# Mixer stage: the scan's result kept token-major until gated, with an order of work of its own for each engine

## The reference

```
x = x + 0.5 * ffn0(layernorm(x));  x = x + attention(layernorm(x));  x = x + 0.5 * ffn0(layernorm(x))
x = x + 0.5 * experts(layernorm(x))          # 8 experts, weighted by how often a gate chooses each
x = x + mixer(layernorm(x))
x = x + 0.5 * experts(layernorm(x))
```

```
proj = x @ W_in                  # split into z (256), x_raw (512), B (128), C (64), dt, lam, theta
x_raw = silu(x_raw); B, C = rms-normed, rotated by angles that are a running sum of dt * theta
y = y_intra + y_inter            # products within a chunk, and with the state carried from chunk to chunk
y = rms(y * silu(z))             # rms over the 256 inner features of a token
return y @ W_out
```

## Time and profile before

| | us |
|---|---|
| three runs: lowest, median, highest | 2490.32, 2500.99, 2504.65 |
| the profiled execution, its own time | 2492.45 |
| its span, first to last instruction | 2490.3 |

### The profile page before, as it was taken

How to read it: one execution, slowest core, us unless ns; L and a number is a source line. 1 busy time by engine, 2 the same in 40 slices (tenths; PEclk the granted TensorE clock), 3 DMA queues, 4 the chain that set the end, 5 groups by cost and what they waited for, 6 DMA issues and landing times. The chain is left out here.

```text
span 2490.3 us, 39953 instructions
## 1 busy us (share of the span) xinstructions
PE 2152.8 (86%) x14226; PEld 986.3 (40%) x14226; DVE 1827.8 (73%) x4240; ACT 1408.9 (57%) x2651; POOL 1448.4 (58%) x1264
## 2 busy tenths in 40 slices
PE   3689889989989989989999998479899898998778
PEld 1223233333333333333333322246566566665534
DVE  5777777777777777777777772368888888887668
ACT  2166666566566566566567566254655555556234
POOL 3366666665675665675665645146556565656358
PEclk9699999999999999999999999699999999999789
DMA  3221121212112112112112110100000000000033
GB/s 118 55 49 39 35 52 43 50 37 52 43 35 64 31 35 65 31 35 64 31 45 50 43 57 9 34 14 22 27 23 26 23 27 22 23 18 18 10 103 109
DMA packets 86599, 103.70 MB, mean 42 GB/s; under 512 B 10241, under 2 KB 68737, under 8 KB 86273
## 3 DMA queue, kind: packets, MB, share of 16 engines
q1 hardware_dynamic: 86400, 101.16, 15.5%
HBM read 29.55 MB, written 20.97 MB: 20 GB/s over the span
## 5 line engine op out<-in xcount | busy, mean ns | idle before, releaser
L386 DVE TENSOR_REDUCE mS<-ps 128x1 f32<-128x512 f32 x1024 | 672.1, 683 | 248.9 <-PE ps L758 243.5
L545 ACT ACTIVATE pr<-ps 128x512 f32<-128x512 f32 x1024 | 586.1, 598 | 382.3 <-PE ps L742 365.7
L615 POOL TENSOR_TENSOR prs<-pr 128x512 f32<-128x512 f32 x384 | 487.1, 1289 | 226.2 <-ACT pr L545 226.2
L758 PE MATMUL ps<-kst,qst 96*128 96x512 f16 x1024 | 393.1, 392 | 64.5 <-DVE mS L386 55.7
L742 PE MATMUL ps<-qst,kst 97*128 97x512 f16 x1024 | 388.7, 387 | 37.1 <-ACT pr L545 35.5
L780 PE MATMUL ps<-pr,vt 128*32 128x512 f32 x2048 | 279.2, 618 | 0.0
L742 PEld LDWEIGHTS ps<-qst,kst 97*128 97x128 f16 x1024 | 97.8, 98 | 372.5 <-ACT pr L545 229.8
L619 POOL TENSOR_TENSOR terms<-terms 128x512 f32<-128x512 f32 x128 | 162.7, 1271 | 99.9 <-DVE terms L379 99.9
L624 POOL TENSOR_TENSOR lo<-terms,hi 128x512 f16<-128x512 f32 x128 | 147.8, 1155 | 81.8 <-ACT hi L525 81.8
L379 DVE TENSOR_TENSOR terms<-ps,shared 128x512 f32<-128x512 f32 x256 | 172.1, 679 | 26.1 <-POOL lo L624 19.8
L758 PEld LDWEIGHTS ps<-kst,qst 96*128 96x128 f16 x1024 | 100.7, 98 | 222.1 <-DVE mS L386 156.2
(11 more groups left out here) (267 smaller groups left out, 4386.6 us busy)
## 6 DMA issues: line engine op xcount, KB each, us to landing
qst<-hi SPq DMA_DIRECT2D x128, 128.0 KB, 2.4
kst<-hi SPq DMA_DIRECT2D x128, 128.0 KB, 2.4
qst<-lo SPq DMA_DIRECT2D x64, 128.0 KB, 2.4
kst<-lo SPq DMA_DIRECT2D x64, 128.0 KB, 2.4
x<-in_q SPq DMA_DIRECT2D x16, 256.0 KB, 3.0
shared<-in_rope SPq DMA_DIRECT2D x1, 4096.0 KB, 14.1
x<-yold SPq DMA_DIRECT2D x16, 256.0 KB, 3.0
n<-kept SPq DMA_DIRECT2D x16, 256.0 KB, 2.1
```

Source lines behind the costliest of these rows:

```text
L386: v.tensor_reduce(mS[:, b % 2, t, s:s + 1], ps[:, 2 + n % 2, :], AX, ALU.max).then_inc(S["s_read"], 1)
L545: a.activation(pr[:, s % 2, g, :], ps[:, g % 2, :], ACT.Exp, scale=ATT_SCALE).then_inc(S["exp"], 1)
L615: g.tensor_tensor(prs[:, c, :], pr[:, 0, c, :], pr[:, 1, c, :], ALU.add).then_inc(S["prs"], 1)
L758: mm(ps[:, 2 + n % 2, :], qst[0:3 * DH, h, P * t:P * t + P], kst[0:3 * DH, h, :], start=True, stop=True).then_inc(S["s"], 1)
```

## The change

Between `products` and `W_out` the data path of a chunk is changed:

- `turn_y` no longer adds. GpSimd adds `pt[0]` and `pt[1]` to `own` in two additions of 128 x 256 (`join`), with a wait for its own first addition between them.
- `z` is projected token-major: `gates` on TensorE makes, for each chunk, three products of 256 columns with the tokens as the stationary operand (12 products of 256 columns a batch in place of 6 of 512), and ScalarE's silu writes `zs` token-major.
- `gated` on VectorE multiplies the joined `own` by `zs`, both in SBUF, into `yz` (two buffers).
- `squares` on ScalarE squares `yz` and sums over the free dimension in the same instruction (`accum_out`); `mean_square` on TensorE goes, and VectorE scales the sums in SBUF.
- `turn_y` is two plain transposes a chunk, and ScalarE copies their result from PSUM to `yzT` (`evacuate_y`, new, 128 x 256).

Besides, the one table becomes four, one for each engine, with places from 0 to 540 in an iteration of 420 (a place of 420 or more falls into the next iteration, so the end of a scan now lies there). Pieces that shared a slot have places of their own on each engine, and some are cut in two (`shift` / `mean_bc`, `angles` / `decays`, `rotate` / `rotate_low`, ScalarE's `decays` / `sin`, the two halves of `states`). `keep_busy` keeps its 5 + 2 products at places of its own. The number of iterations is written as 20; the last has no work left in it. The semaphores of a stage need no longer have adjoining numbers (`clear_semaphores`).

```diff
-    "wo": 1, "out": 3, "stats_gate": 3, "xn_gate": 5, "turn_gate": 15, "gate": 16, "top": 16,
-    "variants": (1, 5, 35, 38), "chunks": (2, 15, 50, 73), "states": (4, 14, 56, 72), "chunks_rest": (7, 22, 66, 74),
-    "products": (7, 22, 65, 75), "own": (1, 2, 26, 58), "own_p": (2, 7, 17, 70), "turn_y": (25, 35, 69, 77),
-    "gated": (34, 44, 73, 80), "squares": (25, 45, 66, 75), "mean": (35, 66, 77, 82), "mean_read": 82,
-    "experts": (15, 17, 22, 25, 36, 44, 59, 64), "sumT": 68, "y": 71, "stats2": 73, "xn2": 74, "turn2": 80,
-    "low2": 82, "project": (1, 2, 3, 6), "gates": 11, "shift": 7, "soft": 15, "steps": 34, "norm_bc": 15, "sums": 41,
-    "angles": 49, "weights": 56, "rotate": 65, "diagonal": 74, "diagonal_p": 71, "bt": 73, "scores": 75, "mask": 78,
+    "DVE": {"out": 150, "stats_gate": 170, "gate": 340, "top": 380, "variants": (10, 60, 110, 210),
+        "states": (30, 50, 140, 160, 260, 280, 370), "products": (120, 220, 350, 420), "gated": (200, 330, 460, 500),
+        "mean_read": 520, "experts": (20, 70, 180, 240), "low": 400, "y": 310, "stats": 320, "shift": 90, "mean_bc": 130,
+        "steps": 190, "decays": 230, "angles": 250, "weights": 270, "rotate": 290, "rotate_low": 300, "diagonal": 360, "mask": 390},
+    "ACT": {"xn_gate": 190, "turn_gate": 220, "own": (60, 130, 240, 280), "squares": (180, 270, 500, 520),
+        "evac_y": (420, 460, 510, 540), "experts": (20, 150, 170, 210), "xn": 260, "turn": 290, "project": (10, 30, 50, 70),
+        "gates": 140, "square_bc": 110, "soft": 160, "decays": 200, "sin": 230, "bt": 250},
+    "POOL": {"own": (10, 30, 130, 140), "join": (40, 100, 150, 420), "experts": (50, 80), "stats_gate": 60, "rms": 440,
+        "stats": 120, "norm_bc": 70, "rotate": 90, "diagonal": 110},
+    "PE": {"wo": 130, "turn_gate": 210, "gate": 250, "chunks": (50, 140, 220, 310), "rest": (100, 180, 290, 320),
+        "turn_y": (330, 440, 490, 530), "experts": (0, 10, 80, 150, 160, 170, 190, 240), "busy": (230, 260), "sumT": 270,
+        "turn": 340, "project": (30, 40, 60, 90), "gates": 120, "sums": 200, "bt": 280, "scores": 300},
...
+        def placed(engine, i, q):
+            def pieces(name, role):
+                at = AT[engine][name]
+                for late in (1, 0):
+                    for k, place in enumerate(at if isinstance(at, tuple) else (at,)):
+                        if place == q + SLOTS * late and batches(i - late)[role] is not None:
+                            yield batches(i - late)[role], k
...
                 def gated(b, t):
-                    dve.wait_ge(S["yT"], upto("yT", b, t + 1))
+                    dve.wait_ge(S["sum"], upto("sum", b, t + 1))
...
-                    v.tensor_tensor(yzT[:, t], ps[:, 5, 0:256].rearrange("p (c m) -> p c m", c=2),
-                                    zsT[:, b % 2, :, P * t:P * t + P], ALU.mult).then_inc(S["yz"], 1)
+                    v.tensor_tensor(yz[:, t % 2, :], own[:, t % 2, 0], zs[:, b % 2, t, :], ALU.mult).then_inc(S["yz"], 1)
...
-                    a.activation(sqy[:, t % 2], yzT[:, t], ACT.Square).then_inc(S["sqy"], 1)
+                    a.activation(sqy[:, t % 2], yz[:, t % 2, :], ACT.Square, accum_out=ms[:, t:t + 1]).then_inc(S["sqy"], 1)
+                def evacuate_y(b, t):
+                    act.wait_ge(S["yT"], upto("yT", b, t + 1))
+                    a.copy(yzT[:, t].rearrange("p c m -> p (c m)"), ps[:, 5, 0:256]).then_inc(S["yzT"], 1)
...
+                def join(b, t):
+                    pool.wait_ge(S["own_w"], upto("own_w", b, t + 1))
+                    pool.wait_ge(S["prod"], upto("prod", b, t + 1))
+                    wait(g.tensor_tensor(own[:, t % 2, 0], own[:, t % 2, 0], pt[:, t % 2, 0], ALU.add))
+                    g.tensor_tensor(own[:, t % 2, 0], own[:, t % 2, 0], pt[:, t % 2, 1], ALU.add).then_inc(S["sum"], 1)
...
-                    for c in range(2):
-                        three_products(ps[:, 3 + c, :], lambda h: w["w_in_hl"][:, h, 512 + P * c:512 + P * c + P],
-                                       lambda l: xhl[:, l, :]).then_inc(S["pr_z"], 1)
+                    for t in range(NT):
+                        ins = three_products(ps[:, 3 + t // 2, D_INNER * (t % 2):D_INNER * (t % 2) + D_INNER],
+                                             lambda h: xhl[:, h, P * t:P * t + P], lambda l: w["w_in_hl"][:, l, 512:768])
+                        if t % 2:
+                            ins.then_inc(S["pr_z"], 1)
...
                     for c in range(2):
-                        for k, part in enumerate((own[:, t % 2, 0], pt[:, t % 2, 0], pt[:, t % 2, 1])):
-                            ins = mm(ps[:, 5, P * c:P * c + P], part[:, P * c:P * c + P], w["ident"][:, :],
-                                     start=k == 0, stop=k == 2)
+                        ins = nc.tensor.transpose(ps[:, 5, P * c:P * c + P], yz[:, t % 2, P * c:P * c + P], w["ident"][:, :])
                     ins.then_inc(S["yT"], 1)
...
-                def mean_square(b, t):
-                    pe.wait_ge(S["sqy"], upto("sqy", b, t + 1))
-                    for c in range(2):
-                        ins = mm(ps[:, 5, 256 + 2 * t:258 + 2 * t], sqy[:, t % 2, c, :], ones[:, :],
-                                 start=c == 0, stop=c == 1, skip_group_check=True)
-                    ins.then_inc(S["ms_mm"], 1)
```

More of the change, by code:

```diff
@@ L32, with clear_semaphores @@
 ATT_SCALE = float((64 / 16) ** -0.5)
+def clear_semaphores(nc, nums):
+    first = nums[0]
+    for n, after in zip(nums, nums[1:] + [None]):
+        if after != n + 1:
+            nc.gpsimd.sem_clear(range(first, n + 1))
+            first = after
 def rope_tables():
@@ L970 @@
-    "low2": 82, "project": (1, 2, 3, 6), "gates": 11, "shift": 7, "soft": 15, "steps": 34, "norm_bc": 15, "sums": 41,
-    "angles": 49, "weights": 56, "rotate": 65, "diagonal": 74, "diagonal_p": 71, "bt": 73, "scores": 75, "mask": 78,
-}
+    "DVE": {
+        "out": 150,
+        "stats_gate": 170,
+        "gate": 340,
+        "top": 380,
+        "variants": (10, 60, 110, 210),
+        "states": (30, 50, 140, 160, 260, 280, 370),
+        "products": (120, 220, 350, 420),
+        "gated": (200, 330, 460, 500),
+        "mean_read": 520,
+        "experts": (20, 70, 180, 240),
+        "low": 400,
+        "y": 310,
+        "stats": 320,
+        "shift": 90,
+        "mean_bc": 130,
+        "steps": 190,
+        "decays": 230,
+        "angles": 250,
+        "weights": 270,
+        "rotate": 290,
+        "rotate_low": 300,
+        "diagonal": 360,
+        "mask": 390,
+    },
@@ new lines @@
+    "ACT": {
+        "xn_gate": 190,
+        "turn_gate": 220,
+        "own": (60, 130, 240, 280),
+        "squares": (180, 270, 500, 520),
+        "evac_y": (420, 460, 510, 540),
+        "experts": (20, 150, 170, 210),
+        "xn": 260,
+        "turn": 290,
+        "project": (10, 30, 50, 70),
+        "gates": 140,
+        "square_bc": 110,
+        "soft": 160,
+        "decays": 200,
+        "sin": 230,
+        "bt": 250,
+    },
+    "POOL": {
+        "own": (10, 30, 130, 140),
+        "join": (40, 100, 150, 420),
+        "experts": (50, 80),
+        "stats_gate": 60,
+        "rms": 440,
+        "stats": 120,
+        "norm_bc": 70,
+        "rotate": 90,
+        "diagonal": 110,
+    },
@@ new lines @@
+    "PE": {
+        "wo": 130,
+        "turn_gate": 210,
+        "gate": 250,
+        "chunks": (50, 140, 220, 310),
+        "rest": (100, 180, 290, 320),
+        "turn_y": (330, 440, 490, 530),
+        "experts": (0, 10, 80, 150, 160, 170, 190, 240),
+        "busy": (230, 260),
+        "sumT": 270,
+        "turn": 340,
+        "project": (30, 40, 60, 90),
+        "gates": 120,
+        "sums": 200,
+        "bt": 280,
+        "scores": 300,
+    },
+}
+MIXER_SLOTS = 420
+UNREAD = (5, 2)
@@ new lines, in _ @@
+                        for b, t in at("chunks", SCAN):
+                            chunk(b, t)
+                        for b, t in at("rest", SCAN):
+                            chunk_rest(b, t)
+                        for b, t in at("turn_y", SCAN):
+                            turn_y(b, t)
+                        for b, e in at("experts", FFN):
+                            expert(b, e)
+                        for b, k in at("busy", FFN):
+                            keep_busy(b, UNREAD[k])
```

445 lines of the change are left out of this document (220 added, 225 removed).

## The result

The changed kernel takes 2430.38 us (median of 4 runs, 2427.29 to 2432.88) against 2498.41 of the kernel before beside it: ratio 0.9729, interval 0.9697 to 0.9761. The forecast was 2437 us, in a range of 2388 to 2488. A second measurement, together with other kernels on another occasion, gave 2430.19 us and a ratio of 0.9730 (0.9717 to 0.9744).

The account below looks back on a forecast made before the run. VectorE's own list of 38.8 us plus 6.7 of waits was taken as the bound. Waits gained 4.9 less contention 1.1 gave 3.8 an iteration, 49.4 for thirteen, plus 6: 55 off 2492.45, so 2437 us; range 2388 to 2488.

Parts of the forecast that it names:

- VectorE's waits: Seven waits of VectorE, 6.7 us an iteration; 1.8 were to stay, a gain of 4.9, bounds 0 and 6.7.
- Contention: GpSimd's additions and VectorE's gatings share the way into SBUF: 1.1 us an iteration lost.
- Filling and draining: Iterations outside the thirteen full ones: 3 us gained in each of two, 0 in the first two and last two.
- Worth nothing by itself, since TensorE is not what ends last: TensorE falls from 41 to about 35 us an iteration; this only loosens VectorE's waits for it.
- waits of order, not of capacity: Six of VectorE's seven waits are for TensorE or ScalarE, which are themselves not full.
- the part with the least room: GpSimd's eight additions, 9.9 us, bring it to 36.8 us, 38.8 with standing still: level with VectorE.
- the rival: GpSimd becomes the bound: its list reaches 47.0 us, 49 with waiting, 3.5 a period more, 2545 us; chance 0.12.
- The wait before the mean: VectorE waits about 1.0 us for ScalarE's squares of the batch before, a new wait replacing the old 1.1.
- the walk: Going through the four new lists by hand, with the iteration's durations, to find which of VectorE's waits stay.
- the wait for GpSimd's half of the rotation: VectorE's copy still follows straight on the rotation: 0.5 of 1.0 us of waiting stays.
- The clock's rival: Emptier TensorE's clock falls once an iteration, products take 2.5 us longer, gain falls to 1.8: 2465 us; chance 0.06.
- The gatings' rival: Each of VectorE's four gatings waits out one GpSimd addition, 2.9 us an iteration, gain 0.9: 2478 us; chance 0.10.

Follow-up runs that it names:

- the kernel that keeps its clock: The changed kernel with 12 more unread products an iteration on TensorE, in its two longest pauses: 2420.95 us, 0.9703 of the kernel before.
- the whole load: The changed kernel with seven unread products on TensorE ahead of each chunk's turn, 28 an iteration, some 6 us: 2519.64 us, 1.0092 of the kernel before.
- the order alone: The kernel before with only the order by engine changed, its data path kept: 2533.64 us, 1.0153 of the kernel before.
- the path only: The kernel before with only the data path changed, all engines keeping the one table of places: 2602.76 us, 1.0427 of the kernel before.

## Why the prediction came out right, and where it was wrong

*The size.* Forecast 3.8 us an iteration, measured 45.52 - 41.06 = 4.46. VectorE's waits: 1.8 left forecast, 1.3 found in a short iteration (2.9 in a long one). Contention: 1.1 forecast, 0.3 found in VectorE's sequence (38.8 before, 39.1 after), 0.7 in its busy time (37.58, 38.25). That small sum hides a shift: the cast of the earlier trace rows takes 269 ns in the mean where it took 1115, while the products that weigh the carried states (L1298) take 466 where they took 286 (L1212 before). With 1.3 of waits and 0.3 of contention the gain would be 5.1; the iterations with a lower clock take back the 0.6 that are missing (by the kernel that keeps its clock, 41.01 - 40.26 = 0.75). Filling and draining: 6 forecast, 12.9 - 5.7 = 7.2 found. The 3.6 us ahead of the mixer were not foreseen; in the second profile of the changed kernel the mixer's first output leaves at 1703.79, 3.9 earlier than in the first, so a difference of this size comes and goes between two profiles of one kernel.

*The step that failed* is the first half of the sentence on TensorE, "Worth nothing by itself, since TensorE is not what ends last". Its second half, that the relief loosens VectorE's waits for TensorE, is what the runs bear out. They put 0.8 us of period on each us of TensorE at the turns, 0.57 in its pauses: putting the 6 us back costs 5.1, more than the 4.5 gained. The reasoning took the engine with the fewest waits for the bound and the other's pauses for room. The waits suggest another picture: TensorE's pauses are waits for VectorE and ScalarE, which had waited for TensorE, a circle in which what is added to one part comes out late at the next. The 7.9 us that VectorE waits under the whole load fit this; no run follows the circle step by step. That VectorE's waits are "waits of order, not of capacity" does not hold in the order tried either: with the order alone, and TensorE as full as before, they come back, 9 us of them on three lines, and taking 3.55 us off TensorE there takes 2.95 off the period. What the prediction had right, that VectorE's waits would go, needed both halves with the places tried: the order, which turns TensorE's relief into earlier results, and the relief, without which the order is 37 us slower than no change. So the time came out near the forecast although one premise of it, that the order alone frees VectorE, was wrong: the change makes both halves at once.

*GpSimd, "the part with the least room".* Its additions take 0.91 and 1.03 us, within 0.8 to 1.4, but its own other work got shorter (25.0 us, where it was 26.9), it is busy 32.8 in place of the 36.8 forecast, and 7.7 us of the iteration stay idle. Its load counts all the same, by another way than the rival had it: eight more additions make VectorE 5.15 us busier. The rival's price (GpSimd's list full) never came.

*The wait before the mean,* forecast at 1.0, is not there: in the iteration from 1831.07 on VectorE needs 8.7 us between `low` and the mean, where the walk had 7.4, and ScalarE's last sum is read 0.2 us before. The wait for GpSimd's half of the rotation is gone too (0.5 forecast).

*The clock's rival* was true in part. It was put at one pause of 1.4 us; there are two, 1.5 and 2.5, and the clock falls behind one of them in ten of thirteen iterations (to a mean of 0.96). In six of the ten it falls behind the pause of 1.5 us and the iteration stays short; in the four long ones it falls behind that of 2.5 us, and VectorE waits. It makes TensorE's work 1.4 to 1.7 us longer where 2.5 were put, and cost 0.75 us an iteration in the mean, not 2.0.

*The gatings' rival:* 523 ns in the mean in place of 417, 0.4 us an iteration and not 2.9.

## What to carry to other kernels

An engine with pauses isn't free: where its pauses are waits for the engine that waits for it, a us taken off it can count (0.5 to 0.9 us here), and unread products measure that price before anything is rewritten. A reordering and a shorter path can each lose alone, as these two did with their tables, and win together, so price the pair. An emptied TensorE can give its gain back as clock; unread products in the pauses kept it here at no visible cost.

## What the runs showed of the hardware that was not expected

A square with a row sum on ScalarE is two instructions, the second, which reads the sum, of 197 ns; the prediction's estimate of 0.2 us was right (groups of the changed kernel):

```profile
L1520 ACT ACTIVATE m_sqy<-m_yz 128x256 f32<-128x256 f32 x52 | 21.8, 418 | 11.1 <-DVE m_yz L1327 11.1
...
L1520 ACT ACTIVATION_READ_ACCUMULATOR m_sqy<-m_yz 128x1 f32 x52 | 10.2, 197 | 0.0
```

GpSimd's power of 4 elements a partition takes 2458 ns in the changed kernel for the mean, and 1036 for the variances:

```profile
L1647 POOL TENSOR_TENSOR m_rms<-m_ms,minus_half 128x4 f32<-128x4 f32 x13 | 32.0, 2458 | 7.4 <-DVE m_ms L1331 7.4
...
L1586 POOL TENSOR_TENSOR m_rstd<-m_veps,minus_half 128x4 f32<-128x4 f32 x26 | 26.9, 1036 | 0.0
```

The first took 1007 ns before, and 1018 with the path only, which has the same operands. So it goes by something around it; what that is stays open. GpSimd has the time.
